# Routing tokens group by group into sorted regions of DRAM, and running the expert matmuls in two waves around the last group's convolution

## The reference

```python
# x: (8, 512, 1024), cond_2048: (8, 1024), all float32
y = causal depthwise conv1d(x, w=cond_2048[:, None, :], 8 taps) + b     # per channel
logits = einsum('bsh,eh->bse', y, w_router)                             # 8 experts
idx = argmax(logits, axis=-1)
out = x + (w_experts[idx] @ y), token by token                          # 1024 x 1024 per expert
```

## Time and profile before

| | |
|---|---|
| median of 3 runs | 687.84 us (686.28 to 688.94) |
| the profiled execution | 687.4 us, of which the span is 685.6 us |
| TensorE busy | 635.6 us (93%), 3058 matmuls; mean granted clock 0.957 |
| VectorE busy | 382.0 us (56%), 345 instructions |
| ScalarE busy | 174.2 us (25%) |
| GpSimd busy | 157.1 us (23%) |
| moved by DMA | 118.13 MB, mean 172 GB/s |

### The profile page before, as it was taken

One profiled execution on the slowest core, in us unless ns is written; L12 is line 12 of the kernel. 1 busy time (PEld: TensorE's weight loads), 2 busy tenths in 40 slices (PEclk: granted clock), 3 DMA queues, 4 the chain that ended last, 5 costly groups with the idle time before them and its releaser, 6 DMA issues.

```text
span 685.6 us, 9583 instructions
## 1 busy us (share of the span) xinstructions
PE 635.6 (93%) x3058; PEld 488.1 (71%) x3059; DVE 382.0 (56%) x345; ACT 174.2 (25%) x199; POOL 157.1 (23%) x206
## 2 busy tenths in 40 slices
PE   1999999999999449999999999999999999999991
PEld 0556566666758338888888888888888888888881
DVE  5699999999999867531217212124411712181710
ACT  2124243323415215510106000014201500060600
POOL 5700000000000140233223332222323332222421
PEclk9989999999997559999999999999999999999996
DMA  8735275275321669574436743344743843476310
GB/s 291 290 124 161 84 246 165 86 238 182 107 78 62 214 206 371 195 287 148 142 122 218 258 144 124 126 135 148 294 144 104 317 156 127 128 277 220 96 65 8
DMA packets 50844, 118.13 MB, mean 172 GB/s; under 512 B 5520, under 2 KB 22032, under 8 KB 50832
## 3 DMA queue, kind: packets, MB, share of 16 engines
q1 hardware_dynamic: 35280, 67.64, 28.2%
q0 software_dynamic: 15552, 50.34, 21.9%
HBM read 89.13 MB, written 35.13 MB: 181 GB/s over the span
## 4 chain that ended last, share of the span: by engine, by line
PE 72%; issue 13%; DVE 9%; DMA 1%; POOL 1%; ACT 1%; SPq 0%; DVEq 0%; POOLq 0%; ACTq 0%
PE ps L626 56%; PE ps L525 8%; DVE y_t L359 6%; PE ps L604 5%; PE ps L547 2%; PE ps L532 1%; POOL diag L653 1%; DMA cst<-consts 1%; DVE x_sb L431 1%; DMA rows<-y_dram,idx 1%; DVE x_sb L428 0%; ACT y_t L277 0%; DVE x_sb L424 0%; DVE ys L478 0%; DVE rows L472 0%
## 5 line engine op out<-in xcount | busy, mean ns | idle before, releaser
L626 PE MATMUL ps<-w_sb,ys 128*128 128x512 f32 x1680 | 395.2, 394 | 0.0
L626 PEld LDWEIGHTS ps<-w_sb,ys 128*128 128x128 f32 x1680 | 314.1, 189 | 67.1
L359 DVE SCALAR_TENSOR_TENSOR y_t<-x_sb,taps,y_t 128x1024 f32<-128x1024 f32 x168 | 203.5, 1288 | 13.6 <-ACT y_t L282 7.0
L478 DVE TENSOR_TENSOR ys<-ps,ys 128x1024 fp32r<-128x1024 f32 x36 | 44.1, 1224 | 260.4 <-ACT ys L323 260.0
L525 PE MATMUL ps<-x_sb,diag 128*128 128x512 f32 x288 | 131.9, 613 | 13.9 <-POOL diag L653 13.9
L323 ACT CAST ys<-ps 128x1024 fp32r<-128x1024 f32 x36 | 36.5, 1014 | 317.6 <-PE ps L604 317.6
L525 PEld LDWEIGHTS ps<-x_sb,diag 128*128 128x128 f32 x288 | 55.1, 196 | 78.4 <-issue 78.4
L532 PEld LDWEIGHTS ps<-wr,y_t 128*128 128x128 f32 x512 | 76.4, 217 | 6.1 <-issue 4.3
L365 DVE TENSOR_TENSOR w_sb<-w_raw,w_sb 128x1024 fp32r<-128x1024 f32 x64 | 76.0, 1222 | 5.2 <-ACT w_sb L298 1.6
L532 PE MATMUL ps<-wr,y_t 128*128 128x8 f32 x512 | 75.6, 229 | 1.6 <-DVE y_t L359 1.6
L547 PE MATMUL ps<-cst,y_t 128*128 128x128 f32 x256 | 71.3, 316 | 0.8 <-ACT rows L292 0.8
(11 more groups left out here) (58 smaller groups left out, 107.5 us busy)
## 6 DMA issues: line engine op xcount, KB each, us to landing
w_raw<-experts SPq DMA_DIRECT2D x64, 512.0 KB, 6.0
x_sb<-x_t SPq DMA_DIRECT2D x32, 512.0 KB, 4.9
y_dram<-rows SPq DMA_DIRECT2D x16, 1024.0 KB, 5.6
rows<-y_dram,idx POOLq DMA_INDIRECT x37, 4.9
rows<-x_rows,idx POOLq DMA_INDIRECT x36, 4.4
out<-rows,idx POOLq DMA_INDIRECT x35, 3.4
cst<-consts SPq DMA_DIRECT2D x1, 377.0 KB, 9.1
cst<-consts SPq DMA_DIRECT2D x1, 64.0 KB, 5.1
```

The costliest lines, as they stand in the source:

```text
L359: nc.vector.scalar_tensor_tensor(out=y, in0=x_sb[:, c, :, k:k + SEQ], scalar=taps[:, c, k:k + 1], in1=y, op0=ALU.mult, op1=ALU.add).then_i ...
L478: nc.vector.tensor_tensor(ys[:, LO, k, :, :].rearrange("p c s -> p (c s)"), turn_both, ys[:, HI, k, :, :].rearrange("p c s -> p (c s)").bi ...
L626: mm = nc.tensor.matmul(out_ps[k][:, f * HALF:(f + 1) * HALF], ys[:, a, k, c, :], w_sb[:, (b * HC + c) * H + f * HALF:(b * HC + c) * H + ( ...
```

## The change

The token rows no longer wait for the whole routing. DRAM holds `y_sorted`, with a region of 4096 rows for each expert, and `id_sorted` for the token numbers. As soon as a group is routed, its 1024 rows are scattered straight to their places in the regions (`place_rows`, `scatter_y`, `scatter_ids`), so that a slot is 128 consecutive rows of a region and is read with plain transfers (`load_y`, four of 128 KB on ScalarE's queue, 1 KB runs). Their layout is such that VectorE's transpose of 32x32 blocks (`turn_blocks`) puts the channels on partitions; the weights' rows are permuted on the host to match. TensorE's `turn` of each slot is gone.

The expert slots come in two waves. The first has 17 slots, the number of full blocks of 128 that the first three groups (`EARLY`) give for any routing. It begins with the expert that had most tokens after two groups, whose weights are loaded ahead. The second wave has the rest, 18 here. Worked out from the counts above: wave one has experts 3 (6 slots), 1 (1), 2 (4), 4 (3) and 5 (3); wave two has 5 (3), 0 (1), 1 (1), 2 (3), 3 (3), 4 (2), 6 (3) and 7 (2). Weights are thus converted 12 times instead of 8.

The last group (`LATE`) has no taps on TensorE. VectorE adds 56 of its taps and ScalarE 8: 4 on VectorE before wave one and 52 in it, five behind each slot (`SLOT_TAPS`). Its logits, transposes and ranks stand behind slots 3, 6, 9, 11, 12 and 13 on TensorE (`BEHIND`).

```diff
-PE_COUNT = [0, 0, 5, 4, 0, 0, 5, 4]
+EARLY = 3
+FIRST_WAVE = -(-(EARLY * TPG * P - EXPERTS * (P - 1)) // P)
+PE_COUNT = [[0, 0, 5, 4, 0, 0, 5, 4]] * EARLY + [[0] * HC] * (GROUPS - EARLY)
...
+        GAP_TAPS = (3, 1)
+        SLOT_TAPS = 5
+        BEHIND = {3: [("logits", 0), ("logits", 1)], 6: [("logits", 2), ("logits", 3)], 9: [("logits", 4), ("logits", 5)],
+                  11: [("logits", 6), ("logits", 7), ("turn", 0), ("turn", 1)],
+                  12: [("rank", 0), ("turn", 2), ("turn", 3), ("turn", 4)], 13: [("turn", 5), ("turn", 6), ("turn", 7)]}
+        CHOOSE_AT, PLACE_AT, TABLE_AT, SCATTER_AT = 12, 13, 14, 13
...
+            def load_y(w, n):
+                row = row_of(w, n)
+                src = y_sorted.rearrange("(r p) n -> r p n", p=P)[bass.ds(row, 1)].rearrange(
+                    "r (t i) (q f) -> (r i) q t f", t=4, q=4)
+                for q in range(4):
+                    nc.scalar.dma_start(y_blk[32 * q:32 * q + 32, :, :, :].rearrange("p t m f -> p t (m f)"),
+                                        src[:, q]).then_inc(y_got, 16)
...
+            for t in range(FIRST_WAVE):
+                w1, n1 = entry(t + 1)
+                w2, n2 = entry(t + 2)
+                high_y(t + 1, (t + 1) % RING, t + 1 < RING)
+                if (w2, n2) == (1, 0):
+                    sorted_is_out(1)
+                load_y(w2, n2)
...
+                load_idx(w1, n1, (t + 1) % IDX_RING, (t + 1 - IDX_RING) // RING + 1 if t + 1 >= IDX_RING else None)
+                high_w(w1, n1, t + 1)
...
+            add_taps(GAP_TAPS[0])
+            choose(EARLY - 1)
+            add_taps(GAP_TAPS[1])
+            place_rows(EARLY - 1)
+            first_table()
+
+            dve.wait_ge(taps_done, TAPS_DONE[EARLY - 1, HC - 1])
+            for c in range(HC):
+                low(0, c)
+            turn_blocks(0, True)
+            low_y(0, 0)
+            for t in range(FIRST_WAVE):
+                w1, n1 = entry(t + 1)
+                k = (t + 1) % RING
+                if t == CHOOSE_AT:
+                    choose(LATE)
+                if t == PLACE_AT:
+                    place_rows(LATE)
+                if t == TABLE_AT:
+                    second_table()
+                turn_blocks(t + 1, False)
+                if t:
+                    residual(t - 1, (t - 1) % RING, (t - 1) // RING + 1)
+                low_y(t + 1, k)
+                add_taps(SLOT_TAPS)
+                low_w(w1, n1)
...
+                scatter_y(g)
+                scatter_ids(g)
+            gather_x(0, 0, 1, None)
+            for t in range(FIRST_WAVE):
+                if t:
+                    scatter(t - 1, (t - 1) % RING, (t - 1) % IDX_RING)
+                gather_x((t + 1) % RING, (t + 1) % IDX_RING, (t + 1) // IDX_RING + 1, (t - 1) // RING + 1 if t else None)
+                if t == SCATTER_AT:
+                    scatter_y(LATE)
+                    scatter_ids(LATE)
+                    fill_rest()
```

More of the change, by code:

```diff
@@ new lines, with x_loads @@
+TAP_ORDER, TAPS_DONE = tap_order()
+X_OWN = 5
+X_SLOT = [[c if g < EARLY else c % X_OWN for c in range(HC)] for g in range(GROUPS)]
+def x_loads(g, c):
+    return sum(X_SLOT[a][b] == X_SLOT[g][c] for a in range(GROUPS) for b in range(HC) if (a, b) <= (g, c))
+C_IDENT, C_ONES = 0, P
+C_FIRST = C_ONES + EXPERTS
+C_BASE = C_FIRST + EXPERTS
+C_EXPERT = C_BASE + EXPERTS
+C_ROW = C_EXPERT + EXPERTS
+C_NTH = C_ROW + EXPERTS
+C_SPLIT = C_NTH + EXPERTS
+C_SLOT = C_SPLIT + TILES + 1
+C_TOKEN = C_SLOT + MOST
@@ new lines, in _, with find_first @@
+            count, first, others, used, start, n_of, flag, nth, more = (per[:, i, :] for i in range(1, 10))
+            resident, room, rest, tmp, tmp2 = (per[:, i, :] for i in range(10, 15))
+            full_row = one[:, 5:6]
+            def find_first():
+                step(V.tensor_tensor(count, base, const(C_BASE), ALU.subtract))
+                step(V.tensor_reduce(one[:, 0:1], count, AX.X, ALU.max))
+                step(V.scalar_tensor_tensor(out=tmp, in0=count, scalar=one[:, 0:1], in1=const(C_FIRST), op0=ALU.is_equal,
+                                            op1=ALU.mult))
+                step(V.tensor_reduce(one[:, 0:1], tmp, AX.X, ALU.max))
+                step(V.tensor_scalar(first, const(C_FIRST), one[:, 0:1], None, ALU.is_equal))
+                step(V.tensor_scalar(one[:, 0:1], one[:, 0:1], -1.0, float(EXPERTS), ALU.mult, ALU.add))
+                step(V.tensor_copy(one_i[:, 0:1], one[:, 0:1]))
+                step(V.tensor_tensor(tmp, first, const(C_ROW), ALU.mult))
+                V.tensor_reduce(full_row, tmp, AX.X, ALU.add).then_inc(first_known, 1)
@@ L498, in _ @@
-            with dve.Fori(1, ROUNDS) as i:
+                        low(nth_load, c)
+            PER_GROUP = [sum(len(dve_taps(g, c)) for c in range(HC)) for g in range(GROUPS)]
+            for g in range(EARLY):
+                if g == 0:
+                    add_taps(PER_GROUP[0])
+                    continue
+                add_taps(5)
+                choose(g - 1)
+                add_taps(7)
+                place_rows(g - 1)
+                if g == EARLY - 1:
+                    find_first()
+                add_taps(PER_GROUP[g] - 12)
@@ new lines, in tokens, with logits @@
+            def tokens(g, c, j):
+                return y_of(g)[:, c, :, :].rearrange("p b s -> p (b s)")[:, j * P:(j + 1) * P]
+            def logits(g, c):
+                pe.wait_ge(taps_done, TAPS_DONE[g, c])
+                if g > 1 and c == 0:
+                    pe.wait_ge(pos_ready, g - 1)
+                for j in range(TPG):
+                    mm = nc.tensor.matmul(logit_ps(g)[:, j, :], tokens(g, c, j), wr[:, c, :], start=(c == 0 and j == 0),
+                                          stop=(c == HC - 1 and j == TPG - 1), skip_group_check=True)
+                mm.then_inc(logit_done, 1)
@@ new lines, in _, with gemm @@
+            g = EARLY - 1
+            logits(g, 6)
+            logits(g, 7)
+            for j in range(2):
+                turn(g, j)
+            rank(g)
+            for j in range(2, 5):
+                turn(g, j)
+            for j in range(5, TPG):
+                turn(g, j)
+            def gemm(t, k, w, n, first):
+                if not first:
+                    nth = pe.value_load(tab_i[0:1, w, 1, bass.ds(n, 1)], min_val=0, max_val=2 * EXPERTS - 1)
+                pe.wait_ge(ys_lo, t + 1)
+                if not (isinstance(t, int) and t < RING):
+                    pe.wait_ge(res_done, t - 1)
+                for c in range(HC):
+                    if first:
@@ L722, in _ @@
-            scatter(last, 0)
-            with pool.If(last < full):
-                scatter(last, 1)
-            pool.wait_ge(row_out[0], (last + 1) * 16)
-            pool.wait_ge(row_out[1], full * 16)
+            for g in range(EARLY):
+                scatter_y(g)
+                scatter_ids(g)
+            gather_x(0, 0, 1, None)
+            for t in range(FIRST_WAVE):
+                if t:
[5 more added lines that the diff above has]
+                    fill_rest()
```

988 lines of the change are left out of this document (549 added, 439 removed).

## The result

The changed kernel takes 749.63 us in the median (748.62 to 752.99, 4 runs) against 687.06 us on the same chip (686.20 to 688.94, 4 runs): a ratio of 1.0915, interval 1.0871 to 1.0959. It is 63 us slower, where a time of 646 us, 42 us faster, was forecast. The profiled execution took 752.99 us with a span of 751.1, so 107 us over the sum of 645.8 have to be found.

A forecast was written before the change was run, and what follows sets the result against it. It took VectorE's taps, with TensorE as full, then routing and first gather, then TensorE's expert matmuls as bounds. First matmul 208, wave one to 429.5, wave two 198 plus 2, tail 14.5 and 1.8 gave 645.8 us; range 633 to 663.

The forecast's parts named there:

- The stage of taps: Three groups: late second-group logits cost VectorE 1.9 us, bounds 0 and 6; the third group's taps end at 176.9.
- the 7.2 us of small steps: Stage of taps: 31 small VectorE steps of choosing, placing and finding the first expert, added ahead of the third group's last tap.
- two equal chains: Gap before the first expert matmul: VectorE's chain ends at 207.4, the row scatters' at 207.5; first matmul at 208, bounds 205 and 214.
- Wave one, 213.6 and 7.9: The 17 slots with logits, transposes and ranks take 213.6 us, plus 7.9 of waits, 2.8 of them at slot 15; ends 429.5.
- The wait ahead of slot 7: Wave one: a second new expert in a row makes TensorE wait 4.0 us for VectorE's low parts of weights.
- come some 3 to 8 us ahead of need: Seam of the waves: slot 17's load and slot 15's gather of x, held by the fills, still arrive in time.
- cost nothing: Wave two, 198 us: eight weight conversions behind a slot are covered by VectorE's spare time, unless weights are late (2 us taken).
- the loop of loads through `y_blk`: Rival, slower than before, 0.06: one buffer's loop, 8.7 us, bounds slots if landings reach 8.7; 732 us at 10 us landings.
- late logits: Stage of taps, 4 us, within the rival that VectorE or this stage is worse than laid out: 658 us, chance 0.17.
- late transfers: Rival: single-slot experts 4 us more, slot 16 or 17 waits 4, first slot 5 later; 659 us, chance 0.15.
- the page's rule: Small transfers are mostly overhead below 64 KB; held against the 128 KB y loads, cost hidden if they land within 8 us.
- the hidden taps of the last group: Wave one covers the last group's taps: 52 done in iteration 10, three slots to spare; the rival against it had 0.04.

The follow-up runs named there:

- e13: The 720.35 us kernel (512-byte token-number rows, index load behind high parts, fills first) with convolution units halved between router matmuls and choosing ten taps late: 710.21 us.
- e15: As e14 without the later choosing (five taps into the next group, places seven behind), convolution units still halved: 710.12 us.
- e1: Changed kernel with the 32 scatters of token numbers left out and the index lists read from an input: 729.16 us, ratio 1.0604.
- e5: Changed kernel with token numbers in rows of 512 bytes instead of 4, initial list fill gone, 8 fill scatters added: 725.27 us, ratio 1.0548.
- e2: Changed kernel with the first expert's eight high parts behind the copies out of the third group on ScalarE: 743.14 us, ratio 1.0807.
- e9: Changed kernel with the edits of e2, e3 and e5 together: 722.63 us, ratio 1.0489.
- e10: As e9, with GpSimd issuing the eight fills of sorted rows ahead of the last group's token-number scatters: 717.06 us, ratio 1.0429.
- e14: As e13, with the first expert's high parts behind the copies out of the third group: 708.71 us, ratio 1.0318.
- e3: Changed kernel with the slot's index load behind the eight high parts of a new expert's weights, both waves: 735.84 us, ratio 1.0701.
- e7: Changed kernel with the y load issued ahead of the high copy of y, once the block transpose has freed its buffer: 762.19 us, ratio 1.1085.
- e6: Changed kernel with the first expert found a group sooner and its raw weights loaded ahead of the third group's x: 758.58 and 772.01 us.
- e8: Changed kernel with the edits of e2, e3, e5, e6 and e7 together: 732.07 us, ratio 1.0682.

## Why the prediction was wrong, point by point

**The stage of taps: VectorE wants the second group's logits at 126.3, TensorE has them at 128.2, wait 1.9.** VectorE took them at 142.9, 14.7 us after the forecast's 128.2. That is nearly all of the 16.6 by which the last tap is late; behind it VectorE pauses once more, for 1.7 us. The order in which TensorE's work was laid out is right, and it ran without a pause over 0.6 us; the step that failed is the price of a matmul. Up to 142.7 the convolution records took 7.8 us more than was counted, and the two groups of router matmuls 36.2 us where 29.0 were counted; transposes and ranks took 10.4 for 10.8. 0.44 a record and 1.8 for a chunk's 16 router records were read at a clock of 1.00. At that clock they hold here too: 32 router matmuls from 107.80 to 111.29, at 1.00, take 3.5 us where 3.6 were counted. But 64 in a row take 10.6 at 0.65, and the units of 16 among the router's runs up to 9.66 in place of 7.1. This made TensorE the bound of the stage, and e13 to e15 show it. The bound of 6 us for this wait was too tight, and the 7.2 us of small steps were nearly right (6.6).

**The gap, 31 us, from "two equal chains".** It was 61.5, the largest error in one place after wave two. By links:

| link | forecast | measured |
|---|---|---|
| last tap to the end of `place_rows` (208.0) | 7.5 | 14.5 |
| to the landing of the last row scatter (229.7) | 13.6 | 21.6 |
| to the landing of the first y block (251.2) | 6 | 21.5 |
| to the first matmul | 4 | 3.9 |

The issues and the pace of GpSimd were counted, but in the sum the 32 id scatters were put at nothing: 128 packets of 4 bytes each. Around them the DMA engines were 0.88 busy at 85 GB/s, the first expert's weights landed 30 us after their last issue, the copies of the third group stood behind ScalarE's high parts for these, and the first y blocks landed 19.0 us after their issue where 4.9 was taken. e1 and e5 shorten the gap by 17 and 16 us, e2 by 5. What is left over the forecast, 12 to 15 us in e5, e9, e10 and e14, was not taken apart by a run: the third group's 96 router matmuls in a row took 17.95 us in e5, at a clock of 0.50 from 184 on, and the first y block landed 11 us after its last issue there.

**Wave one, 213.6 and 7.9.** The wait ahead of slot 7 was forecast as 4.0 and is 3.91, and VectorE's iteration holds: there is no other wait in the ten tap slots. Slot 15 waits 4.62 in place of 2.8. The step that failed is that the load of slot 17 and the gather for slot 15 "come some 3 to 8 us ahead of need" behind `fill_rest`. The last fill landed 14.88 us after its issue where 3.4 was taken, the load behind it took 8.40, and slot 17 could not start before 504.98, 39.3 us behind slot 15, where two slots take 22. The 11 us by which stutter stretches slots 15 and 16 lie inside this time and cost nothing here: TensorE was through them at 499.0, and slot 17's block was landed only at 501.17. Of the 28.4 us the seam makes 17.3 and slot 15's wait 1.8; most of the rest are slots and logits at a clock of 0.75 to 0.96.

**Wave two, where the conversions "cost nothing".** They cost 25.3 us of waits. The comparison of 9.3 us of low parts with a slot of 11 was right; what was left out is the loop in which they stand: block transpose, high part of y, four issues and two register loads and an index load on ScalarE (4.95), eight high parts (7.7), the last low part, and on VectorE the next block transpose behind it, 17.5 us for a slot of 11. e3 takes one link out, and wave two is 13.5 us shorter: 10 in waits and the rest in slots that no longer start slow. The other 9 of the 34.3 us that the wave is over its forecast are slots of 11.0 to 11.9 and one of 13.1, where 11.0 each and 2 for late weights had been counted.

**The rivals.** The one on the other side, the loop of loads through `y_blk`, named the right symptom with the wrong link: landings have a median of 4.1 in e5, under the 8.7 from which it decides, and e7, which has the loads issued earlier, only made it slower. That its 732 us lie nearest to the measured time is luck. Two rivals with smaller prices named places that did cost: late logits, at 4 us, and late transfers, with the first slot 5 later and slot 16 or 17 waiting 4. By the Trainium skill ("DMA: Bandwidth & Descriptors", Rules for kernel authors) transfers under 64 KB are mostly overhead. The prediction held the page's rule against the 128 KB loads, which cost little by e5 once the small packets were gone. The trace agrees with it for the id scatters, of 512 bytes each.

**Right**: the block transpose at 1.24 (1.2), the wait ahead of slot 7, the hidden taps of the last group (TensorE waits for none of them), the tail within 3.

**What stays open.** e14 is still 21 us over the kernel before. By its rows the gap is 44.2 (31.1 forecast), wave one about 251 (221.5) and wave two 219 (200): wave one is no shorter than in the changed kernel. Most of it stands at the seam: some 43 us from the start of slot 15 (433.24) to that of slot 17 (about 476). VectorE ended the low part for slot 17 at 472.6, after a wait of 9.6 for a gather of x; so the pauses of the stutter, 12.8 us in all, can have cost about 4 there. The second table adds 4.6. No run moved the gathers of x ahead of the scatters. The cause of the stutter is open. It has no releaser and lies where scatters and fills are in flight, but e1, with the fills and no id scatters, and e5, e6, e7 and e8, with both, don't have it:

```profile
442.88 23.67 PE L857 MATMUL ps<-w_sb,ys 128*128 128x512 f32 x96 [4.59 <-DVE ys L674]
476.75 45.79 PE L857 MATMUL ps<-w_sb,ys 128*128 128x512 f32 x192 [10.19 <-DVE ys L674]
```

These are slots 15 and 16 of e5 and the four behind them. A run without fills wasn't tried, since rows never written would be read.

## What to carry to other kernels

Price a matmul at the clock that its new neighbours leave: here, taking the wide matmuls away from between the router's, and opening pauses in a stage of slots that had none, was paid on the matmuls behind them too. Price an indirect transfer by how small its packets are, not by its bytes, and ask what else is in flight while they drain. When a conversion is called covered, write down the whole ring of engines it stands in, issues and register loads included, and compare the ring's length with the slot's, not each engine's busy time. And before a pause is put into the bill, ask what the next step was waiting for: the stutter looks like 11 us and costs none in the changed kernel.

## What the runs showed of the hardware

- 128 packets of 4 bytes in an indirect scatter cost far more than 128 of 512 bytes: DMA share 0.88 at 85 GB/s against 0.01 at 2 GB/s in the same stretch, and 24 us of the kernel (e5).
- A pause lengthens what comes behind it. A slot of 48 matmuls took 13.12 us after 6.22 of waiting, at a granted clock of 0.84, and 11.20 after 1.63, at 1.00 (e3). The stage of slots, at a granted clock of 1.00 from 300 to 400 before, had 0.90 there and 0.94 from 505 to 551.
- Router matmuls of 8 columns in a long row go with a low granted clock, though TensorE has no pause: 64 took 10.76 at 0.65, while 32 at 1.00 took 3.63. Where in the stage the clock is low differs between executions of the same order (last tap at 187.2 to 195.0).
- While 16 scatters and 8 fills were issued or in flight, TensorE started single matmuls, mostly 1.4 to 2.9 us apart, with nothing to wait for, in the changed kernel and ten others; in e5, with as many, it did not.
